# State space stage of a two-layer decoder: exponentials left in PSUM banks, matrix products on VectorE, terms on GpSimd

## The chip, the cores and the metric

The kernel runs on one core of one Trainium2 chip. The metric is the device time of one execution in microseconds. The kernel before was timed in three runs: 2670.41, 2675.45 and 2675.78 us, median 2675.45 us. The profile is of one more execution.

## What is computed

A decoder of two layers works on x, 16 batches of 256 tokens by 256 features in fp32, with a layer norm after every sublayer. The sublayers are: differential self attention, cross attention, a mixture of experts, a state space layer (Mamba-2 style), causal cross attention and a LoRA feed forward. The change touches the state space layer alone:

```python
zxbcdt = jnp.einsum('bld,ed->ble', x, in_proj_w)      # z 512, xBC 768, dt 8
xBC = silu(causal depthwise conv(xBC, 4 taps) + conv_b)
dt = softplus(dt + dt_bias);  A = -exp(A_log)          # 8 heads of 64, state of 128
...
def step(state, inp):
    x_t, B_t, C_t, dt_t = inp
    decay = jnp.exp(A[None, :] * dt_t)
    state = state * decay[:, :, None, None] + (x_t * dt_t[:, :, None])[..., None] * B_t[:, None, None, :]
    y_t = jnp.einsum('bhpn,bn->bhp', state, C_t)
...
y = (y + x_part * D) * silu(z)
y = y * rsqrt(mean(y * y) + EPS) * norm_w
x = layernorm(x + y @ out_proj_w.T)
```

## The kernel before

The recurrence is not stepped. With a = A dt, the output of a batch is y[t] = sum over s <= t of exp(a[s+1] + ... + a[t]) (B[s] . C[t]) dt[s] x[s]. For each batch and head the kernel makes the matrix of these factors and multiplies the scaled rows by it. The 256 tokens make two blocks of 128, so there are three blocks of matrix (first by first, first by second, second by second), and the eight heads are cut in two halves of four. That gives six units u = 0 to 5 a batch: block u // 2, half u % 2. Every unit is 128 x 512.

A unit goes through these steps. `high_terms` and `low_terms` multiply a triangle by a, split in an upper part `a_hi` and a rest `a_lo`, one tile of 128 x 1024 for each block of tokens (q = 0, 1); these are `rhs_hi` (VectorE) and `rhs_lo` (GpSimd). `exponents(n, u)` (TensorE) sums them by two matmuls into one of two banks, `e_ps[u % 2]`. `decays(n, u)` (ScalarE) takes the exponential from the bank and writes it to `mat[:, u]` in SBUF. `matrices(eng, n, u, ready)` multiplies `mat[:, u]` in place by `gm`, the masked products B . C, on VectorE for u = 0, 2, 4 and on GpSimd for u = 1, 3, 5. `mix(n, blk)` (TensorE) multiplies the scaled rows `xdt` by `mat`. A bank is free again once ScalarE has read it, and the same two banks also carry the transposed rows (`to_rows`) from which `scaled_rows` makes `xdt`.

Around it runs the rest of the layer. Inputs are projected for two batches at a time in eleven units (B, C, x0, x1, x2, dt, x3, z0 to z3) into two other banks, `in_ps`: six units in the even step, five in the odd. `project(n, i)` waits in `free_bank` until the unit two before it has been read out of its bank: for B, C and x units by the third tap of the convolution on VectorE (`taps`), which follows `first_tap` on ScalarE. `time_steps` and `exponent_terms` make dt and `a_hi`, `a_lo` for a pair of batches in the odd step; `copy_steps` (ScalarE) and `turn_steps` (TensorE) bring the dt unit to rows. Ahead of that, GpSimd gathers the expert rows of a batch by four indirect DMAs (`gather`), VectorE sums them and takes row moments (`sum_experts`), GpSimd makes the inverse root and `c_shift` (`scale_x`), ScalarE normalizes (`normalize_x`), and TensorE transposes the rows. Behind it, `output` multiplies by the output weights, `mean_squares`, `scale_rows`, `residual`, `row_moments`, `scale_y` and `normalize_y` finish a batch, and `skip_terms`, `gated`, `upper_y`, `square_y` and `split_y` lie between `mix` and the next step's `output`.

The order is written out by hand: each engine has a loop over the steps n = -7 to 16, with one order for even and one for odd n, and every engine runs its queue strictly in that order, with semaphores between the engines. A step handles batch n (`now`), finishes batch n - 1 (`late`) and prepares n + 1 (`soon`), while projections run for the pair that starts at n + 2, `normalize_x` for n + 4, `scale_x` for n + 5 and `gather` for n + 7. What can't be read from the diff is ScalarE's order in an even step, which doesn't change:

```python
first_tap(n, 0); decays(n, 0); first_tap(n, 1); normalize_x(n + 4)
decays(n, 1); decays(n, 2); tails(n); decays(n, 3)
first_tap(n, 2); decays(n, 4); first_tap(n, 3); decays(n, 5); first_tap(n, 4)
split_x(n + 4); upper_y(n); square_y(n); normalize_y(n - 1); copy_steps(n)
```

TensorE's order in an even step is `project(n, 0)`, `state_products`, `exponents` 0 and 1, `project(n, 1)`, `exponents` 2 and 3, `project(n, 2)`, `exponents` 4 and 5, `project(n, 3)`, `output(n - 1)`, `mix`, `project(n, 4)`, `transpose_x`, `to_rows(n + 1)`, `project(n, 5)`; the odd step has `turn_steps` ahead of its projections, and two of them between the exponents.

## Time and profile before

| What | us |
|---|---|
| median of three runs (2670.41 to 2675.78) | 2675.45 |
| the profiled execution | 2671.63 |
| its span, first to last instruction | 2669.9 |
| VectorE, GpSimd, ScalarE, TensorE busy in the span | 1950.1, 1619.4, 1423.5, 2341.5 |
| products with the mask, L2827, on VectorE (48 of them), median of one | 0.790 |
| the same on GpSimd (48), median of one | 1.312 |
| exponentials, L2670, ScalarE (96), median of one | 0.594 |
| first and last exponential of the stage start at | 1654.1, 2018.4 |

The mean granted clock of TensorE is 0.937 of full speed over the span. In the trace PE is TensorE, DVE is VectorE, ACT is ScalarE, POOL is GpSimd. Instructions overlap a little at their ends, so that from the start of one to the start of the next can be less than its duration. In a merged row, x2 says that two instructions in a row are counted, and the time is that of both. Idle time before a row stands in brackets, with what ended it.

### The profile page before, as it was taken

How to read it: one execution, taken by the hardware profiler on the slowest of the kernel's cores; microseconds unless marked ns; L12 is line 12 of the kernel's file. 1: busy time of each engine (PE TensorE's matmuls, PEld its weight loads, DVE VectorE, ACT ScalarE, POOL GpSimd, SP SyncE). 2: the span in 40 equal slices, each digit the busy share in tenths (PEclk: the TensorE clock that was granted, in tenths of full speed). 3: DMA queues.
4: the chain of work that ended last, by engine and by line, in shares of the span. 5: the costliest groups of instructions: out<-in, count | busy, mean ns of one | idle time of the engine just before them, and what ended most of it. 6: DMA issues, size and time to landing. Idle time of an engine off the chain costs nothing. (4 is left out here: it accounts for less than half of the span.)

```text
span 2669.9 us, 63255 instructions
## 1 busy us (share of the span) xinstructions
PE 2341.5 (88%) x23480; PEld 1968.6 (74%) x23480; DVE 1950.1 (73%) x3223; ACT 1423.5 (53%) x2223; POOL 1619.4 (61%) x1937
## 2 busy tenths in 40 slices
PE   5999999997799877998999965988995899987998
PEld 4677777775566656998999964777774666756998
DVE  2677777776589872646888857999984588875776
ACT  2566666664466652335666544655652466653333
POOL 3667666764467751275666656777764587863443
PEclk9899999999899987999999987998996799988999
DMA  8566666551889841146666652111002887841111
GB/s 205 131 159 159 160 145 158 153 120 43 245 216 229 219 111 36 52 138 204 224 228 226 230 175 64 41 48 32 21 13 85 213 225 208 224 105 41 53 54 52
DMA packets 227288, 363.44 MB, mean 136 GB/s; under 512 B 51968, under 2 KB 156416, under 8 KB 219520
## 3 DMA queue, kind: packets, MB, share of 16 engines
q1 hardware_dynamic: 207392, 281.32, 39.7%
q0 software_dynamic: 17376, 78.13, 8.6%
q8 instruction: 143, 2.34, 0.4%
q10 hardware_dynamic: 2304, 1.05, 0.2%
q14 instruction: 73, 0.60, 0.1%
HBM read 231.72 MB, written 133.69 MB: 137 GB/s over the span
## 5 line engine op out<-in xcount | busy, mean ns | idle before, releaser
L1369 ACT ACTIVATE self_probs<-self_score_ps 128x768 f32<-128x768 f32 x256 | 208.7, 815 | 183.9 <-PE self_score_ps L1271 182.0
L1585 POOL TENSOR_SCALAR_AFFINE_SELECT self_probs<-self_probs 128x512 f32<-128x512 f32 x256 | 169.5, 663 | 158.6 <-ACT self_probs L1369 158.6
L1506 DVE TENSOR_REDUCE self_neg_max<-self_max_ps 128x2 f32<-128x256 f32 x256 | 108.1, 422 | 165.1 <-PE self_max_ps L88 165.1
L647 ACT ACTIVATE cross_probs<-cross_score_ps 128x1024 f32<-128x1024 f32 x128 | 131.2, 1025 | 101.6 <-PE cross_score_ps L545 100.0
L745 DVE TENSOR_REDUCE cross_neg_max<-cross_max_ps 128x4 f32<-128x1024 f32 x128 | 154.9, 1212 | 39.1 <-PE cross_max_ps L524 39.0
L1507 DVE TENSOR_REDUCE self_neg_max<-self_max_ps 128x2 f32<-128x512 f32 x256 | 174.5, 682 | 0.0
L2297 POOL TENSOR_TENSOR moee_h_lo<-moee_h,moee_h_hi 128x512 fp32r<-128x512 f32 x78 | 112.5, 1442 | 92.3 <-ACT moee_h_hi L2034 91.6
L739 DVE TENSOR_REDUCE causal_block_max<-causal_max_ps 128x6 f32<-128x768 f32 x128 | 120.9, 946 | 56.4 <-PE causal_max_ps L88 55.9
L3592 POOL TENSOR_TENSOR ffn_g_lo<-ffn_g_full,ffn_g_hi 128x512 fp32r<-128x512 f32 x64 | 82.1, 1283 | 129.2 <-ACT ffn_g_hi L3478 116.9
L2034 ACT ACTIVATE moee_h_hi<-moee_h 128x512 fp32r<-128x512 f32 x110 | 69.6, 632 | 163.2 <-DVE moee_h L2200 163.2
L647 ACT ACTIVATE causal_probs<-causal_score_ps 128x768 f32<-128x768 f32 x128 | 103.6, 809 | 99.2 <-PE causal_score_ps L545 99.0
L79 PE MATMUL moee_g_ps<-moee_x_hi,moee_in_hi 128*128 128x256 f32 x440 | 131.3, 298 | 10.0 <-DVE moee_x_lo L2187 5.8
L1271 PE MATMUL self_score_ps<-self_q_stack,self_k_stack 49*128 49x128 f32 (+1 forms) x1024 | 129.0, 330 | 10.0 <-ACT self_probs L1369 6.4
L2200 DVE TENSOR_TENSOR moee_h<-moee_u_ps,moee_silu 128x512 f32<-128x512 f32 x110 | 75.5, 686 | 82.0 <-PE moee_u_ps L81 77.4
L2240 POOL DMA_INDIRECT x_tiles<-kept_x,moek_slot x64 | 65.8, 1029 | 107.1 <-issue 104.1
L79 PE MATMUL moee_y_ps<-moee_out_hi,moee_h_hi 128*128 128x256 f32 x440 | 125.4, 285 | 0.7 <-DVE moee_out_lo L2152 0.7
L81 PE MATMUL moee_g_ps<-moee_x_hi,moee_in_lo 128*128 128x256 f32 x440 | 125.7, 286 | 0.0
L79 PE MATMUL moee_u_ps<-moee_x_hi,moee_in_hi 128*128 128x256 f32 x440 | 125.7, 286 | 0.0
L80 PE MATMUL moee_g_ps<-moee_x_lo,moee_in_hi 128*128 128x256 f32 x440 | 125.7, 286 | 0.0
L80 PE MATMUL moee_u_ps<-moee_x_lo,moee_in_hi 128*128 128x256 f32 x440 | 125.1, 284 | 0.0
L81 PE MATMUL moee_u_ps<-moee_x_hi,moee_in_lo 128*128 128x256 f32 x440 | 125.1, 284 | 0.0
L81 PE MATMUL moee_y_ps<-moee_out_hi,moee_h_lo 128*128 128x256 f32 x440 | 124.9, 284 | 0.0
(507 smaller groups left out, 9479.9 us busy)
## 6 DMA issues: line engine op xcount, KB each, us to landing
self_q<-self_q_split SPq DMA_DIRECT2D x48, 512.0 KB, 3.5
self_q_raw<-self_q SPq DMA_DIRECT2D x32, 768.0 KB, 8.2
cross_stacks<-cross_qk SPq DMA_DIRECT2D x64, 384.0 KB, 6.4
causal_stacks<-causal_qk SPq DMA_DIRECT2D x64, 384.0 KB, 6.4
moe_y_tiles<-lasting_y_out SPq DMA_DIRECT2D x55, 256.0 KB, 2.5
mid<-lasting_y_out SPq DMA_DIRECT2D x48, 256.0 KB, 2.2
x_tiles<-zeros SPq DMA_DIRECT2D x16, 624.0 KB, 5.5
moee_xT<-x_tiles SPq DMA_DIRECT2D x39, 256.0 KB, 7.3
```

The lines of the kernel that those rows point to most:

```text
L79: pe.matmul(out, a[0], b[0], start=start, stop=False, **kw)
L80: pe.matmul(out, a[0], b[1], start=False, stop=False, **kw)
L81: return pe.matmul(out, a[1], b[0], start=False, stop=stop, **kw)
L647: nc.scalar.activation(probs[i // 2][:, a, :, lo:], score_ps[:, :, lo:], ACT.Exp, scale=HD ** -0.5).then_inc(prob_ready, 1)
L739: last = dve.tensor_reduce(block_max[:, :, col % 4, :], bank[:, :, 0:3 * P].rearrange("p a (j t) -> p a j t", t=P), AX.X, ALU.max, negate= ...
L745: last = dve.tensor_reduce(neg_max[p][:, tile, :, col % 4, :], bank[:].rearrange("p a (q k) -> p a q k", q=QT), AX.X, ALU.max, negate=True)
L1271: last = pe.matmul(score_ps[:, ab, j * S + k * P:(j + 1) * S], k_stack[p][rows, tile, k * P:(k + 1) * P], q_stack[rows, 4 * tile + c, k * P:],
L1369: nc.scalar.activation(probs[g % 4][:, a, :, P:], score_ps[:, :, P:], ACT.Exp, scale=HD ** -0.5).then_inc(prob_ready, 1)
L1506: dve.tensor_reduce(neg_max[:, tile, :, c, 0:1], bank[:, :, 0:P], AX.X, ALU.max, negate=True)
L1507: dve.tensor_reduce(neg_max[:, tile, :, c, 1:2], bank[:, :, S:2 * S], AX.X, ALU.max, negate=True).then_inc(max_kept, 1)
L1585: pool.affine_select(diagonal, diagonal, [[0, 2], [0, 2], [1, P]], ALU.is_ge, zero, base=0, channel_multiplier=-1).then_inc(prob_masked, 1)
L2297: pool.tensor_tensor(h_lo[p][f][:].rearrange("p j s -> p (j s)"), h[f][:], h_hi[p][f][:].bitcast(F32).rearrange("p j s -> p (j s)"), ALU.s ...
```

## The change

- `decays` writes the exponential back to its own bank instead of to `mat`, and no longer waits for `mix` of the batch before.
- `matrices` is VectorE's alone, for all six units. It reads the bank and `gm` and writes `mat[:, u]`; the first of a batch waits for `mix` of the batch before.
- The two counters `low_mat_ready` and `high_mat_ready` become one, `mat_ready`. TensorE's `exponents` (u >= 2) and `to_rows` now wait for it, that is for VectorE's reading of the bank, where they waited for ScalarE's.
- `high_terms` is taken from VectorE; GpSimd makes both rows of terms in `terms`, upper ahead of lower for each q, in the places of `low_terms`. GpSimd makes no product any more.
- VectorE's order changes: in an even step the products stand in pairs ahead of, between and behind the first two chunks of taps, and `sum_experts` moves from the head of the step behind `tail_rows`; in an odd step the products stand in pairs too.

```diff
@@ -2518,7 +2518,7 @@
                 if u >= 2:
-                    pe.wait_ge(decay_ready, 6 * n + u - 1)
+                    pe.wait_ge(mat_ready, 6 * n + u - 1)
                 else:
@@ -2530,7 +2530,7 @@
                     if b:
-                        pe.wait_ge(decay_ready, 6 * b - 1 + q)
+                        pe.wait_ge(mat_ready, 6 * b - 1 + q)
                     for f in range(FT):
@@ -2541,7 +2541,7 @@
                     pe.wait_ge(yd_ready, 2 * n - 1 + blk)
-                pe.wait_ge((low_mat_ready, high_mat_ready)[blk], 3 * n + 3)
+                pe.wait_ge(mat_ready, 6 * n + 5 + blk)
                 t = xdt[n % 2]
@@ -2665,10 +2665,7 @@
                 act.wait_ge(e_done, 6 * n + u + 1)
-                if u == 0 and n:
-                    act.wait_ge(ssm_done, 2 * n)
-                nc.scalar.activation(mat[:, u, :, :].rearrange("p h t -> p (h t)"), e_ps[u % 2][:],
-                                     ACT.Exp).then_inc(decay_ready, 1)
+                nc.scalar.activation(e_ps[u % 2][:], e_ps[u % 2][:], ACT.Exp).then_inc(decay_ready, 1)
 
@@ -2821,12 +2818,6 @@
 
-        def matrices(eng, n, u, ready):
-            eng.wait_ge(decay_ready, 6 * n + u + 1)
-            eng.wait_ge(gm_ready, n + 1)
-            eng.tensor_tensor(mat[:, u, :, :], mat[:, u, :, :],
-                              gm[:, u // 2, :].unsqueeze(1).broadcast_to([P, 4, P]), ALU.mult).then_inc(ready, 1)
-
         @block.vector
@@ -2923,19 +2914,10 @@
 
-            def high_terms(b):
-                if b:
-                    dve.wait_ge(e_done, 6 * b)
-                for q in range(QT):
-                    dve.tensor_tensor(rhs_hi[:, q, :, :], upto.unsqueeze(1).broadcast_to([P, NH, P]),
-                                      a_hi[:, b % 2 * QT + q, :].bitcast(F32).unsqueeze(2).broadcast_to([P, NH, P]),
-                                      ALU.mult).then_inc(rhi_ready, 1)
-
             def masked_products(n):
                 dve.wait_ge(g_done, n + 1)
                 if n:
-                    dve.wait_ge(low_mat_ready, 3 * n)
-                    dve.wait_ge(high_mat_ready, 3 * n)
+                    dve.wait_ge(mat_ready, 6 * n)
                 dve.tensor_tensor(gm[:], g_ps[:, 0:S + P].rearrange("p (b t) -> p b t", t=P), gmask,
@@ -2978,6 +2960,16 @@
                 moments(b, y_out[p], stats, mv[p], stat_ready, mean_ready)
+
+            def matrices(n, u):
+                dve.wait_ge(decay_ready, 6 * n + u + 1)
+                if u == 0:
+                    dve.wait_ge(gm_ready, n + 1)
+                    if n:
+                        dve.wait_ge(ssm_done, 2 * n)
+                dve.tensor_tensor(mat[:, u, :, :], e_ps[u % 2][:].rearrange("p (h t) -> p h t", t=P),
+                                  gm[:, u // 2, :].unsqueeze(1).broadcast_to([P, 4, P]),
+                                  ALU.mult).then_inc(mat_ready, 1)
 
@@ -3008,20 +3000,21 @@
                 if n % 2 == 0:
+                    if now:
+                        masked_products(n)
+                        matrices(n, 0)
+                        matrices(n, 1)
+                    taps(n, 0)
+                    if now:
+                        matrices(n, 2)
+                        matrices(n, 3)
+                    taps(n, 1)
+                    if now:
+                        matrices(n, 4)
+                        matrices(n, 5)
+                        tail_rows(n)
                     if real(n + 5) and n != -2:
                         sum_experts(n + 5)
-                    if now:
-                        masked_products(n)
-                    taps(n, 0)
-                    taps(n, 1)
-                    if now:
-                        matrices(dve, n, 0, low_mat_ready)
-                        matrices(dve, n, 2, low_mat_ready)
-                        tail_rows(n)
-                    if n >= 0 and soon:
-                        high_terms(n + 1)
-                    if now:
-                        matrices(dve, n, 4, low_mat_ready)
                     taps(n, 2)
@@ -3048,17 +3041,20 @@
                         masked_products(n)
+                        matrices(n, 0)
+                        matrices(n, 1)
                     if real(n + 5):
                         sum_experts(n + 5)
                     if now:
-                        matrices(dve, n, 0, low_mat_ready)
-                        matrices(dve, n, 2, low_mat_ready)
+                        matrices(n, 2)
+                        matrices(n, 3)
                         tail_rows(n)
                     taps(n, 0)
+                    if now:
+                        matrices(n, 4)
+                        matrices(n, 5)
                     if late:
                         mean_squares(n - 1)
-                    if now:
-                        matrices(dve, n, 4, low_mat_ready)
                     if late:
@@ -3073,7 +3069,6 @@
                         scaled_rows(n + 1)
-                        high_terms(n + 1)
 
@@ -3119,11 +3114,14 @@
 
-            def low_terms(b, q):
+            def terms(b, q):
                 if q == 0:
                     pool.wait_ge(alo_ready, b // 2 + 1)
                     if b:
                         pool.wait_ge(e_done, 6 * b)
+                pool.tensor_tensor(rhs_hi[:, q, :, :], upto.unsqueeze(1).broadcast_to([P, NH, P]),
+                                   a_hi[:, b % 2 * QT + q, :].bitcast(F32).unsqueeze(2).broadcast_to([P, NH, P]),
+                                   ALU.mult).then_inc(rhi_ready, 1)
                 pool.tensor_tensor(rhs_lo[:, q, :, :], upto.unsqueeze(1).broadcast_to([P, NH, P]),
@@ -3143,17 +3141,12 @@
                 now, late, soon = real(n), real(n - 1), real(n + 1)
-                if now:
-                    matrices(pool, n, 1, high_mat_ready)
-                    matrices(pool, n, 3, high_mat_ready)
                 if n % 2 == 0:
-                    if now:
-                        matrices(pool, n, 5, high_mat_ready)
                     if late:
                         scale_rows(n - 1)
                     if n >= 0 and soon:
-                        low_terms(n + 1, 0)
-                        low_terms(n + 1, 1)
+                        terms(n + 1, 0)
+                        terms(n + 1, 1)
                     if late:
@@ -3166,18 +3159,16 @@
                         scale_rows(n - 1)
-                    if now:
-                        matrices(pool, n, 5, high_mat_ready)
                     if n == -5:
                         scale_x(n + 5)
                     if n == -3:
                         scale_x(n + 5)
                     if soon:
-                        low_terms(n + 1, 0)
+                        terms(n + 1, 0)
                     if late:
                         scale_y(n - 1)
                     if soon:
-                        low_terms(n + 1, 1)
+                        terms(n + 1, 1)
                     if real(n + 7):
```

VectorE's queue, from the end of an odd step into an even one; `ssm_gm` is the masked product of `masked_products`, `ssm_bc` rows are `taps`, `ssm_mat` rows are `matrices`, `ssm_xdt_tail` is `tail_rows`. Before:

```order
L2859 BN_AGGR ssm_c_mv<-ssm_c_stats 128x2 x2
L2939 TENSOR_TENSOR ssm_gm<-ssm_g_ps,ssm_triang 128x384
L2893 SCALAR_TENSOR_TENSOR ssm_bc<-ssm_in_ps,ssm_cw,ssm_bc 128x2x255
L2893 SCALAR_TENSOR_TENSOR ssm_bc<-ssm_in_ps,ssm_cw,ssm_bc 128x2x254
L2893 SCALAR_TENSOR_TENSOR ssm_bc<-ssm_in_ps,ssm_cw,ssm_bc 128x2x253
L2893 SCALAR_TENSOR_TENSOR ssm_bc<-ssm_in_ps,ssm_cw,ssm_bc 128x2x255
L2893 SCALAR_TENSOR_TENSOR ssm_bc<-ssm_in_ps,ssm_cw,ssm_bc 128x2x254
L2893 SCALAR_TENSOR_TENSOR ssm_bc<-ssm_in_ps,ssm_cw,ssm_bc 128x2x253
L2827 TENSOR_TENSOR ssm_mat<-ssm_mat,ssm_gm 128x512 x2
L2947 TENSOR_TENSOR ssm_xdt_tail<-ssm_xdt,ssm_tail 128x512
L2930 TENSOR_TENSOR ssm_rhs_hi<-ssm_triang,ssm_a_hi 128x1024 x2
L2827 TENSOR_TENSOR ssm_mat<-ssm_mat,ssm_gm 128x512
```

With the change:

```order
L2937 TENSOR_TENSOR ssm_xdt<-ssm_e_ps,ssm_dt 128x512 x2
L2921 TENSOR_TENSOR ssm_gm<-ssm_g_ps,ssm_triang 128x384
L2970 TENSOR_TENSOR ssm_mat<-ssm_e_ps,ssm_gm 128x512 x2
L2884 SCALAR_TENSOR_TENSOR ssm_bc<-ssm_in_ps,ssm_cw,ssm_bc 128x2x255
L2884 SCALAR_TENSOR_TENSOR ssm_bc<-ssm_in_ps,ssm_cw,ssm_bc 128x2x254
L2884 SCALAR_TENSOR_TENSOR ssm_bc<-ssm_in_ps,ssm_cw,ssm_bc 128x2x253
L2970 TENSOR_TENSOR ssm_mat<-ssm_e_ps,ssm_gm 128x512 x2
L2884 SCALAR_TENSOR_TENSOR ssm_bc<-ssm_in_ps,ssm_cw,ssm_bc 128x2x255
L2884 SCALAR_TENSOR_TENSOR ssm_bc<-ssm_in_ps,ssm_cw,ssm_bc 128x2x254
L2884 SCALAR_TENSOR_TENSOR ssm_bc<-ssm_in_ps,ssm_cw,ssm_bc 128x2x253
L2970 TENSOR_TENSOR ssm_mat<-ssm_e_ps,ssm_gm 128x512 x2
L2929 TENSOR_TENSOR ssm_xdt_tail<-ssm_xdt,ssm_tail 128x512
```

The first two products now follow `ssm_gm` at once, and six tap instructions that stood ahead of every product stand behind them; `ssm_rhs_hi` is gone, and the sums of the experts, which ended at the first row of before, come after the last row.

GpSimd's queue in an odd step; `ssm_row_scale` is `scale_rows`, `ssm_var` to `ssm_shift` is `scale_y`, the DMAs are `gather`, `ssm_c_var` begins `scale_x`. Before:

```order
L3120 TENSOR_TENSOR ssm_row_scale<-ssm_ms,ssm_neg_half 128x2
L2827 TENSOR_TENSOR ssm_mat<-ssm_mat,ssm_gm 128x512
L3127 TENSOR_TENSOR ssm_rhs_lo<-ssm_triang,ssm_a_lo 128x1024
L3097 TENSOR_SCALAR ssm_var<-ssm_mv 128x2
L3098 TENSOR_SCALAR ssm_low<-ssm_mv 128x2
L3100 TENSOR_TENSOR ssm_rstd<-ssm_var,ssm_neg_half 128x2
L3102 TENSOR_TENSOR ssm_shift<-ssm_low,ssm_rstd 128x2
L3127 TENSOR_TENSOR ssm_rhs_lo<-ssm_triang,ssm_a_lo 128x1024
L3089 DMA ssm_y_routed<-moe_y_tiles,moek_slot 128x256 x4
L3097 TENSOR_SCALAR ssm_c_var<-ssm_c_mv 128x2
L3098 TENSOR_SCALAR ssm_c_low<-ssm_c_mv 128x2
```

With the change:

```order
L3115 TENSOR_TENSOR ssm_row_scale<-ssm_ms,ssm_neg_half 128x2
L3122 TENSOR_TENSOR ssm_rhs_hi<-ssm_triang,ssm_a_hi 128x1024
L3125 TENSOR_TENSOR ssm_rhs_lo<-ssm_triang,ssm_a_lo 128x1024
L3092 TENSOR_SCALAR ssm_var<-ssm_mv 128x2
L3093 TENSOR_SCALAR ssm_low<-ssm_mv 128x2
L3095 TENSOR_TENSOR ssm_rstd<-ssm_var,ssm_neg_half 128x2
L3097 TENSOR_TENSOR ssm_shift<-ssm_low,ssm_rstd 128x2
L3122 TENSOR_TENSOR ssm_rhs_hi<-ssm_triang,ssm_a_hi 128x1024
L3125 TENSOR_TENSOR ssm_rhs_lo<-ssm_triang,ssm_a_lo 128x1024
L3084 DMA ssm_y_routed<-moe_y_tiles,moek_slot 128x256 x4
L3092 TENSOR_SCALAR ssm_c_var<-ssm_c_mv 128x2
L3093 TENSOR_SCALAR ssm_c_low<-ssm_c_mv 128x2
```

A product has gone from behind `ssm_row_scale`, and each `ssm_rhs_lo` has an `ssm_rhs_hi` of the same size ahead of it, both pairs ahead of the gathers and of `scale_x`.

## Rows read from the trace of the kernel before

**Rows 1.** Windows view of one pair of batches: busy us of each engine, clock, DMA.
```profile
1752.00:1802.00 50.00, 43.79 (x306) 37.10 (x306) 47.99 (x88) 30.24 (x48) 38.42 (x40) 0.97 0.15 43
```

**Rows 2.** VectorE groups by shape, 1700 to 1990 us: busy, mean ns, idle before.
```profile
L2827 DVE TENSOR_TENSOR ssm_mat<-ssm_mat,ssm_gm 128x512 f32<-128x512 f32 x36 | 40.0, 1133 | 3.2 <-ACT ssm_mat L2670 2.9
L2930 DVE TENSOR_TENSOR ssm_rhs_hi<-ssm_triang,ssm_a_hi 128x1024 fp32r<-128x1024 f32 x22 | 30.3, 1417 | 1.8 <-PE ssm_e_ps L2527 1.8
```

**Rows 3.** GpSimd groups by shape, 1700 to 1990 us.
```profile
L2827 POOL TENSOR_TENSOR ssm_mat<-ssm_mat,ssm_gm 128x512 f32<-128x512 f32 x36 | 52.1, 1460 | 29.5 <-ACT ssm_mat L2670 28.5 <-DVE ssm_gm L2939 0.6
L3127 POOL TENSOR_TENSOR ssm_rhs_lo<-ssm_triang,ssm_a_lo 128x1024 fp32r<-128x1024 f32 x24 | 45.3, 1896 | 5.7 <-DVE ssm_a_lo L2924 5.7
```

**Rows 4.** Timeline of ScalarE, even step from 1752 us: start, us, instruction, wait.
```profile
1752.25 1.09 ACT L2731 ACTIVATE ssm_x<-ssm_x,ssm_c_shift,ssm_c_rstd 128x256 f32<-128x256 f32 x2 [1.73 <-POOL ssm_c_shift L3102]
...
1759.90 0.78 ACT L2689 ACTIVATE ssm_xs<-ssm_in_ps,ssm_cb,ssm_cw 128x512 f32<-128x512 f32 x1 [1.83 <-PE ssm_in_ps L81]
1760.58 0.59 ACT L2670 ACTIVATE ssm_mat<-ssm_e_ps 128x512 f32<-128x512 f32 x1
```

**Rows 5.** Timeline of GpSimd, odd step from 1788 us.
```profile
1788.46 1.90 POOL L3127 TENSOR_TENSOR ssm_rhs_lo<-ssm_triang,ssm_a_lo 128x1024 fp32r<-128x1024 f32 x1 [0.90 <-DVE ssm_a_lo L2924]
...
1792.66 1.90 POOL L3127 TENSOR_TENSOR ssm_rhs_lo<-ssm_triang,ssm_a_lo 128x1024 fp32r<-128x1024 f32 x1
1794.72 1.87 POOL L3089 DMA_INDIRECT ssm_y_routed<-moe_y_tiles,moek_slot  x1 [0.16 <-issue]
...
1802.04 0.18 POOL L3102 TENSOR_TENSOR ssm_c_shift<-ssm_c_low,ssm_c_rstd 128x2 f32<-128x2 f32 x1
```

**Rows 6.** Timeline of VectorE, from 1761 us.
```profile
1761.40 2.30 DVE L2893 SCALAR_TENSOR_TENSOR ssm_xs<-ssm_in_ps,ssm_cw,ssm_xs 128x510 f32<-128x510 f32 x3
...
1770.91 1.26 DVE L2955 TENSOR_TENSOR ssm_xdt<-ssm_e_ps,ssm_dt 128x512 f32<-128x512 f32 x2
1772.08 2.30 DVE L2893 SCALAR_TENSOR_TENSOR ssm_xs<-ssm_in_ps,ssm_cw,ssm_xs 128x510 f32<-128x510 f32 x3
...
1774.90 0.18 DVE L2905 TENSOR_TENSOR ssm_v<-ssm_in_ps,ssm_bias 128x32 f32<-128x32 f32 x1
...
1775.46 1.91 DVE L2867 SCALAR_TENSOR_TENSOR ssm_y_shared<-ssm_y_routed,moek_weight,ssm_y_shared 128x256 f32<-128x256 f32 x2
...
1780.45 0.68 DVE L2947 TENSOR_TENSOR ssm_xdt_tail<-ssm_xdt,ssm_tail 128x512 f32<-128x512 f32 x1
...
1783.35 2.37 DVE L2827 TENSOR_TENSOR ssm_mat<-ssm_mat,ssm_gm 128x512 f32<-128x512 f32 x1
1786.40 0.88 DVE L2971 SCALAR_TENSOR_TENSOR lasting_y_out<-ssm_xT_ps,ssm_row_scale,ssm_x 128x256 f32<-128x256 f32 x2 [0.68 <-issue]
...
1788.19 0.19 DVE L2924 TENSOR_TENSOR ssm_a_lo<-ssm_a,ssm_a_hi 128x32 fp32r<-128x32 f32 x1
...
1796.69 0.87 DVE L2867 SCALAR_TENSOR_TENSOR ssm_y_shared<-ssm_y_routed,moek_weight,ssm_y_shared 128x256 f32<-128x256 f32 x2
...
1799.47 0.52 DVE L2939 TENSOR_TENSOR ssm_gm<-ssm_g_ps,ssm_triang 128x384 f32<-128x384 f32 x1
```

**Rows 7.** Timeline of TensorE: exponents of even batches; output of an odd step.
```profile
1657.51 0.50 PE L2526 MATMUL ssm_e_ps<-ssm_rhs_hi,ssm_one_r 128*128 128x512 f32 x1 [1.86 <-ACT ssm_mat L2670]
...
1753.87 0.50 PE L2526 MATMUL ssm_e_ps<-ssm_rhs_hi,ssm_one_r 128*128 128x512 f32 x1 [3.72 <-ACT ssm_mat L2670]
...
1779.46 0.28 PE L79 MATMUL ssm_xT_ps<-ssm_wo_hi,ssm_y_hi 128*128 128x256 f32 x1
...
1783.95 0.28 PE L81 MATMUL ssm_xT_ps<-ssm_wo_hi,ssm_y_lo 128*128 128x256 f32 x1
...
1803.89 0.79 PE L2526 MATMUL ssm_e_ps<-ssm_rhs_hi,ssm_one_r 128*128 128x512 f32 x1 [3.72 <-ACT ssm_mat L2670]
...
1904.58 0.50 PE L2526 MATMUL ssm_e_ps<-ssm_rhs_hi,ssm_one_r 128*128 128x512 f32 x1 [1.87 <-ACT ssm_mat L2670]
...
1949.74 0.50 PE L2526 MATMUL ssm_e_ps<-ssm_rhs_hi,ssm_one_r 128*128 128x512 f32 x1 [0.90 <-ACT ssm_mat L2670]
```

2 lines of the change are left out of this document (1 added, 1 removed).

## Prediction

> **What bounds the stage now.** I read first the windows of one pair of batches (one even and one odd step): of 50.00 us VectorE is busy 47.99, TensorE 43.79, GpSimd 38.42, ScalarE 30.24 [rows 1]. VectorE is the fullest engine, so the next view is its groups by shape: 36 products with the mask at 1133 ns and 22 upper terms at 1417 ns on average [rows 2]. These means hide two prices. A product that meets GpSimd's own takes 2.37 us, where a free one takes about 0.7 [rows 6]. The reader sees an engine that is full and partly held up by GpSimd.
>
> The third view, the timelines, shows a second thing that an average can't: a ring through all engines that just fits into the 50 us. In an odd step VectorE ends `a_lo` at 1788.38 [rows 6]. GpSimd starts its lower terms behind it at 1788.46, does `scale_y`, the second lower terms at 1792.66, four gathers from 1794.72, `scale_x`, and ends `c_shift` at 1802.22 [rows 5]: 13.8 us. `normalize_x` of the next even step waits for that `c_shift` on ScalarE (1.73 us in the pair before, start at 1752.25) [rows 4]; behind it in ScalarE's queue stands the second exponential of that batch, and TensorE waited 3.72 us for it, to 1753.87, and again to 1803.89 [rows 7]. In between VectorE did other work, since its queue had ten independent things ahead of the first product; it lost nothing. I call the end of `c_shift` ahead of an even step T0 (1752.2, then 1802.2).
>
> **What the change does to busy time.** VectorE now does 12 products a pair instead of 6, each with one operand in a bank. The nearest row is `scaled_rows`, which multiplies a bank by a broadcast SBUF operand: two begin at 1770.91 and the next work at 1772.08, 0.59 us each [rows 6]. So 12 x 0.59 = 7.1 us. It drops 6 x 1.13 = 6.8 and 4 x 1.42 = 5.7 us [rows 2]. Net 5.4 us a pair less. GpSimd drops 6 products at 1.46 = 8.8 us and gains 4 upper terms, priced as its lower terms of the same shape, 1.90, so 7.6 us [rows 3]: about even. ScalarE's exponential keeps its 0.59 us [rows 4] in my sum. A write to a bank is not in this trace; I bound it by 0.4 and 0.8 us, and since only the second and sixth exponentials stand in the ring, that is +-0.4 us a pair. The Trainium skill ("ScalarE: Activation LUTs", the section on what each stage is for) says that ScalarE writes PSUM faster than SBUF and gives no figure; by it the sum would lie nearer the lower end, and no run shown here tests it.
>
> **What it does to the ring.** Three edits lengthen it.
> 1. GpSimd now makes upper and lower terms between `a_lo` and `c_shift`: 2 x 1.90 = 3.8 us more. Against that, the 1.87 us first gather [rows 5] lay beside VectorE's upper terms, and without them I take 1.0, and `scale_y` loses a stall of some 0.6 beside the gated product. 13.8 + 3.8 - 0.9 - 0.3 = 16.4 us.
> 2. VectorE's queue in an even step now has `matrices(n, 1)` ahead of all taps. It waits for the second exponential, so for `normalize_x`, so for T0. Nothing behind it can start: in-order. Hence all of VectorE's work up to `a_lo` follows T0 in series. `normalize_x` and the exponential take 1.7 us. Then, even step: five products 2.9, two chunks of taps 4.4, tail row 0.6, `sum_experts` 2.8 (1796.69 to 1799.47), and from the third taps to the end 13.5 less 0.4 of idle (1761.40 to 1774.90). Odd step: 0.6 to 1775.46, six products 3.5, `sum_experts` 2.8, tail row with taps 2.9 (1780.45 to 1783.35), residual to `a_lo` 2.0 (1786.40 to 1788.38) [rows 6]. Sum 1.7 + 23.8 + 11.8 = 37.3 us. With GpSimd's 16.4 the ring is 53.7 us if VectorE never waits otherwise, against 50.0.
> 3. It does wait. A bank is free only when VectorE has read it, and the products stand between the taps. Laid out from T0: second product done 2.4, first taps 4.6, two products 5.8, second taps 8.0, fifth product 8.6. TensorE may project `x1` only when the second taps have freed its bank, 8.0 to 9.4; `first_tap` 0.8 and the sixth exponential 0.6 [rows 4] end at 10.9, so VectorE stands 2.3 us before its sixth product. In the trace of before the same exponential already trails that `first_tap` (start 1760.58), but only GpSimd waited. GpSimd's four terms in a row (7.6 us) now lie beside `gated`, the tail row and `sum_experts`: I add 1.4 us for two meetings. The trace shows such meetings: two additions of `sum_experts` took 1.91 us at 1775.46 and 0.87 at 1796.69 [rows 6]. `scale_y` and `normalize_y` come behind these terms and ahead of `copy_steps`: 0.4 us at `time_steps`. In the odd step TensorE gets the banks of the last two exponent units only after `sum_experts`, starts `output` some 1.9 us later, and `output` lasts 4.8 us (1779.46 to 1784.23) [rows 7], so that `residual` waits another 1.3. Sum 5.4. Ring: 53.7 + 5.4 = 59 us.
>
> What hides the lost VectorE time otherwise: between `a_lo` and the next `matrices(n, 1)` VectorE has 6.6 us of work and then stands some 10 us for T0. Its 5.4 us saved go there, and give nothing back.
>
> **The sum.** From the second exponent matmul pair of batch 0 to that of batch 12 the trace has 1657.51 to 1949.74, 292.2 us [rows 7]. After: the first T0 comes 3.8 us of terms later, less the gather's 0.9, of which 1.7 us remain behind the wait that was there; the first ring has no older batch, 55.4; then three at 59, batches 2 to 8, 177.0; the ring from 8 to 10 has no gathers (-5.2) and is then held by the products themselves, 54.2; from 10 to 12 there is no `sum_experts` in the odd step and no `normalize_x` ahead, 51.8. Total 1.7 + 55.4 + 177.0 + 54.2 + 51.8 = 340.1, which is 47.9 us more. From batch 12 on neither taps of a new pair nor inputs remain, and I see gains and new waits of about 1 us that cancel: 0. Other stages are untouched. The profiled execution took 2671.63 us, 3.8 below the median of the three runs shown, so 2671.6 + 48 = **2720 us**. About 0.2% (5 us) is what a measurement of this kernel can tell from none.
>
> **Rivals.**
> *A cheaper ring, still slower.* If the waits of point 3 overlap, the ring is 53.7 us: three rings give 11, the first, fifth and sixth 0 to 2 each, the start 1.7, together 10 to 20 us: 2682 to 2692. For it: the layout above sums waits by hand, and one late engine often covers another. Against: the sixth product's wait has no cover.
> *VectorE's relief wins.* If T0 came before VectorE's queue reached the second product, the pair would shrink by up to 5.4 us, stopped by TensorE's 43.79 of 50 [rows 1], say 4.5 us over seven pairs: -31, 2640 us. It needs `a_lo` at most 33.6 us after T0 (50 less 16.4); before it was 36.2 (1752.2 to 1788.4), and VectorE's own work after T0 is 37.3. That is 3.7 us short of the turning point, so it needs GpSimd's upper terms at half my price. For it only: VectorE is 96% busy now and is what most waits lead to.
> *The shared port decides.* In this trace an instruction of VectorE with two SBUF operands waits for the end of GpSimd's (2.37 us, above). GpSimd's terms now fill 15.2 us a pair, so `gated`, two tail rows and four additions may each wait up to 1.9. At four full waits the ring is 59 + 6 = 65 us and the time 2672 + 72 = 2744. The Trainium skill ("SBUF — State Buffer", who interferes with whom) calls this an exclusive lock for the whole instruction, and says that a VectorE instruction with one SBUF input is exempt. The trace agrees on both: the free bank products of `scaled_rows` keep 1.26 us for two [rows 6].
>
> That the change isn't what it says can be left out: both listings show all twelve products on VectorE and all terms on GpSimd.
>
> **How the numbers follow.** Forecast (ring of 57 to 61 us, 2705 to 2730) 0.55; cheaper ring 0.18, of which 0.03 falls within 0.2%; port 0.12; relief 0.10; anything else near zero change 0.05. Slower 0.82, same 0.08, faster 0.10. The range 2683 to 2748 leaves out the relief and a little of either edge.
>
> **What would show it.** Right: the busy time of VectorE in the stage falls while its idle time before `ssm_mat<-ssm_e_ps` for ScalarE's exponential grows to several us, six times; `c_shift` to `c_shift` near 59 us over the middle pairs; TensorE idle before the exponents for VectorE's products; ScalarE's longest wait is `normalize_x` for `ssm_c_shift`; products near 0.68 us with hardly a spread. Wrong: pairs of 50 us or less, VectorE still over 90% busy, or products of over 0.8 us.

## The result, and the profile after

The changed kernel takes **2762.82 us** (median of 4 runs, 2755.97 to 2763.74) against 2674.36 us for the kernel before (the three runs above and a fourth): a ratio of 1.0329, 95% interval 1.0315 to 1.0344, so 88 us more. The forecast was 48 us more: it had the direction and the chain over `c_shift`, which I call the ring, but the result lies above its range. The profiled execution took 2763.59 us (span 2761.9), 92.0 more than that of before.

How long the **stage** takes is read from each trace in the same way: from the first statistics of an input batch (`ssm_c_mv`) to the first matmul of the next stage. Before it is 502.5 us, after 584.8: 82.3 more. Of the other 9.7 us, 7.8 lie ahead of the stage, in code that the change doesn't touch. The stage began anywhere between 1600.7 and 1610.1 us in the traces below, so I take those 7.8 for spread between executions. The stretches of the prediction, from the TensorE timeline of after (start and duration in us, engine, line, operation, count, idle before and its releaser), second exponent pair of batches 0, 2, 8, 10 and 12:

```profile
1666.65 0.53 PE L2526 MATMUL ssm_e_ps<-ssm_rhs_hi,ssm_one_r 128*128 128x512 f32 x1 [2.55 <-DVE ssm_mat L2970]
...
1727.50 0.79 PE L2526 MATMUL ssm_e_ps<-ssm_rhs_hi,ssm_one_r 128*128 128x512 f32 x1 [4.67 <-DVE ssm_mat L2970]
...
1912.30 0.79 PE L2526 MATMUL ssm_e_ps<-ssm_rhs_hi,ssm_one_r 128*128 128x512 f32 x1 [4.67 <-DVE ssm_mat L2970]
...
1970.58 0.65 PE L2526 MATMUL ssm_e_ps<-ssm_rhs_hi,ssm_one_r 128*128 128x512 f32 x1 [1.49 <-DVE ssm_mat L2970]
...
2026.15 0.51 PE L2526 MATMUL ssm_e_ps<-ssm_rhs_hi,ssm_one_r 128*128 128x512 f32 x1 [0.55 <-DVE ssm_mat L2970]
```

| stretch | before | forecast | after |
|---|---|---|---|
| start, inside the stage | 0 | +1.7 | +1.3 |
| batch 0 to 2 | 46.3 | 55.4 | 60.9 |
| 2 to 8, three rings | 151.6 (1703.82 to 1855.39) | 177.0 | 184.8 |
| 8 to 10 | 49.2 | 54.2 | 58.3 |
| 10 to 12 | 45.2 | 51.8 | 55.6 |
| 12 to the stage's end | 0 | +0 | +13.7 |

The windows view of one ring of after, from one `c_shift` to the next (columns as in [rows 1]):

```profile
1786.81:1848.41 61.60, 48.09 (x306) 37.80 (x306) 43.81 (x89) 30.51 (x48) 36.73 (x39) 0.89 0.12 35
```

VectorE's busy time fell from 47.99 [rows 1] to 43.81 us, the pair rose by 11.6. No engine is full: the pair is a chain. The waits of after from 1720 to 1840 (engine and line, what it waits for: total, times, longest) name its links:

```profile
POOL ssm_row_scale L3115 <- DVE ssm_ms L2944: 38.2, 4, 16.4
...
DVE ssm_mat L2970 <- ACT ssm_e_ps L2668: 20.5, 8, 4.8
...
PE ssm_e_ps L2526 <- DVE ssm_mat L2970: 13.5, 6, 4.7
...
ACT ssm_x L2728 <- POOL ssm_c_shift L3097: 6.1, 2, 3.0
...
PE ssm_xT_ps L2453 <- DVE lasting_y_out L2953: 4.6, 2, 2.3
DVE ssm_gm L2921 <- PE ssm_g_ps L2513: 4.6, 1, 4.6
```

ScalarE waits for `c_shift`, VectorE's product for ScalarE, TensorE's exponent for the product. This is the foreseen chain. The last two rows are not in my layout: in an even step TensorE's `transpose_x` stands 2.3 us for the `residual` of VectorE's queue, and VectorE 4.6 us for TensorE's `g_ps` ahead of the masked products. Step by step, first from the timelines of ScalarE and VectorE of after:

```profile
1786.84 1.09 ACT L2728 ACTIVATE ssm_x<-ssm_x,ssm_c_shift,ssm_c_rstd 128x256 f32<-128x256 f32 x2 [3.04 <-POOL ssm_c_shift L3097]
```
```profile
1788.45 0.69 DVE L2970 TENSOR_TENSOR ssm_mat<-ssm_e_ps,ssm_gm 128x512 f32<-128x512 f32 x1 [4.78 <-ACT ssm_e_ps L2668]
...
1799.13 0.69 DVE L2970 TENSOR_TENSOR ssm_mat<-ssm_e_ps,ssm_gm 128x512 f32<-128x512 f32 x1 [2.60 <-ACT ssm_e_ps L2668]
...
1810.07 2.82 DVE L2994 TENSOR_TENSOR ssm_yz<-ssm_yz,ssm_zs 128x1024 f32<-128x1024 f32 x1
...
1831.40 0.19 DVE L2915 TENSOR_TENSOR ssm_a_lo<-ssm_a,ssm_a_hi 128x32 fp32r<-128x32 f32 x1
...
1842.28 0.56 DVE L2921 TENSOR_TENSOR ssm_gm<-ssm_g_ps,ssm_triang 128x384 f32<-128x384 f32 x1 [4.57 <-PE ssm_g_ps L2513]
```

and GpSimd's leg, in the same view:

```profile
1831.69 1.89 POOL L3122 TENSOR_TENSOR ssm_rhs_hi<-ssm_triang,ssm_a_hi 128x1024 fp32r<-128x1024 f32 x1 [2.38 <-DVE ssm_a_lo L2915]
...
1841.84 1.08 POOL L3084 DMA_INDIRECT ssm_y_routed<-moe_y_tiles,moek_slot  x1 [0.16 <-issue]
...
1848.20 0.19 POOL L3097 TENSOR_TENSOR ssm_c_shift<-ssm_c_low,ssm_c_rstd 128x2 f32<-128x2 f32 x1
```

From T0 (1786.8) to the second product 1.6 us (forecast 1.7), to the sixth 12.3 (10.9), to the end of `a_lo` 44.8 (42.7), and GpSimd from there to `c_shift` 16.8 (16.4). The first gather costs 1.08 us, where I took 1.0.

### The profile page after: what moved, and what is told of

Read it like the earlier page. It is cut to its first block and busy times, and to the rows that moved or that the text cites. A ratio compares the mean times of both kernels' runs of the same rounds, so it can differ in the third digit from the quotient of the medians.

```text
span 2761.9 us, 63160 instructions
## 1 busy us (share of the span) xinstructions
PE 2372.3 (86%) x23480; PEld 1977.7 (72%) x23480; DVE 1920.2 (70%) x3239; ACT 1425.5 (52%) x2223; POOL 1606.5 (58%) x1921
## 5 line engine op out<-in xcount | busy, mean ns | idle before, releaser
L3583 POOL TENSOR_TENSOR ffn_g_lo<-ffn_g_full,ffn_g_hi 128x512 fp32r<-128x512 f32 x64 | 82.3, 1286 | 128.5 <-ACT ffn_g_hi L3469 116.1
L80 PE MATMUL moee_y_ps<-moee_out_lo,moee_h_hi 128*128 128x256 f32 x440 | 124.8, 284 | 0.0
```

The lines of the kernel that those rows point to most:

```text
L80: pe.matmul(out, a[0], b[1], start=False, stop=False, **kw)
```

## Experiments

Each kernel is the one named, with the shown edit alone. The table has what was measured. A pair is the mean of the three even steps from batch 4 to 10, from the masked products of one even step to those of the next. "Beside" is the kernel before in the same session. All but the last two kernels had one execution, so a total is known to some 8 us (the kernel before, 23 times in the last session, ran from 2661.34 to 2680.15), while the stage is steadier: one kernel profiled twice had 498.6 and 499.7. Its last part is the least steady: from the masked products of batch 14 to those of batch 15 the kernel before took 17.3 us and e7_before_norm_late, whose code is the same there, 20.4; e6_before_terms_pool and e14_terms_norm, also the same there, took 21.6 and 26.3. So a difference of under some 5 us between two stages says little.

| kernel | stage | pair | total | beside |
|---|---|---|---|---|
| before | 502.5 | 50.8 | 2671.63 | |
| after | 584.8 | 61.5 | 2763.59 | |
| e1_norm_late | 565.4 | 56.5 | 2745.17 | 2681.85 |
| e2_gather_late | 570.3 | 58.2 | 2743.31 | 2681.85 |
| e4_exp_to_sbuf | 581.6 | 62.7 | 2749.34 | 2681.85 |
| e5_taps_first | 582.0 | 59.8 | 2755.97 | 2681.85 |
| e8_sum_first | 571.8 | 59.2 | 2744.11 | 2673.78 |
| e9_sum_norm | 547.5 | 54.4 | 2725.56 | 2673.78 |
| e3_high_on_dve | 565.1 | 58.1 | 2736.07 | 2673.78 |
| e6_before_terms_pool | 527.0 | 55.4 | 2704.95 | 2673.78 |
| e12_and_steps | 568.3 | 58.8 | 2739.60 | 2674.24 |
| e14_terms_norm | 521.2 | 53.3 | 2698.15 | 2674.24 |
| e7_before_norm_late | 505.9 | 50.8 | 2676.86 | 2674.24 |
| e15_before_order | 529.3 | 54.3 | 2699.13 | 2674.24 |
| e16_sn_sbuf | 545.0 | 54.7 | 2716.71 | 2680.80 |
| e17_sn_high | 532.9 | 52.5 | 2703.85 | 2680.80 |
| e18_hybrid | 503.6 | 49.4 | 2673.63 | 2680.80 |
| e19_hybrid_norm | 498.6 | 48.3 | 2666.76 | 2680.80 |

**The ring over `c_shift`.** In the changed kernel, `normalize_x` of even steps late:

```diff
                     first_tap(n, 1)
-                    if real(n + 4):
-                        normalize_x(n + 4)
...
                         decays(n, 5)
+                    if real(n + 4):
+                        normalize_x(n + 4)
```

> The changed kernel with one move: in even steps ScalarE normalizes the rows of batch n + 4 behind the sixth exponential, not ahead of the second. The state space stage (first row moments to the first attention matmul behind it) took 502.5 us before and 584.8 us with the change. Theory A, the ring through c_shift: the second exponential no longer waits for T0, but it still stands behind the first tap of unit C, which ended 2.4 us ahead of T0. So the second product starts some 2.5 us after T0 less 5, that is 2.5 us earlier, in six steps, and TensorE's wait there falls from 4.7 to about 2.2 us: 15 to 20 us less, stage 565 to 570. Rival B, bank release and product order alone set the pair: no wait moves but TensorE's by under 1 us a pair, stage 578 or more. Rival C, the shared port: no change, 585.

19.4 us of stage less, as my theory said. But the pair stays at 56.5 us: with `c_shift` out of it there is a second ring, nearly as long. Its links are the two that I had not laid out (waits of e1 from 1720 to 1960):

```profile
DVE ssm_mat L2970 <- ACT ssm_e_ps L2668: 23.0, 16, 2.5
...
DVE ssm_gm L2921 <- PE ssm_g_ps L2513: 18.2, 4, 4.6
...
PE ssm_xT_ps L2453 <- DVE lasting_y_out L2953: 9.2, 4, 2.3
```

The same ring, shortened instead of cut: in odd steps GpSimd issues its gathers behind `scale_x`.

```diff
-                    if real(n + 7):
+                    if n < -1 and real(n + 7):
                         gather(n + 7)
                     if n >= -1 and real(n + 5):
                         scale_x(n + 5)
+                    if n >= -1 and real(n + 7):
+                        gather(n + 7)
```

> The changed kernel with one move: from step -1 on, GpSimd's four gathers of an odd step stand behind scale_x. c_shift comes 5.2 us earlier. Theory A: the same 2.5 us a pair as with the late normalization, since then the first tap of unit C bounds the second exponential, so stage 565 to 570, and both experiments agree within 3 us. If they agree, T0 is worth that much and no more of the 82 us. Rival B or C: 578 or more.

14.5 us less, 3.3 us a middle pair, though the four gathers took 5 us ahead of `scale_x`; 4.9 us of stage fewer than with `normalize_x` late, so the two don't agree as closely as A had it. Both say that the c_shift ring holds the changed kernel by no more than 3 to 5 us a pair.

**Banks.** Exponentials go to SBUF as before, ScalarE frees the bank, VectorE multiplies all six in place:

```diff
-                nc.scalar.activation(e_ps[u % 2][:], e_ps[u % 2][:], ACT.Exp)...
+                nc.scalar.activation(mat[:, u, :, :]..., e_ps[u % 2][:], ACT.Exp)...
-                    pe.wait_ge(mat_ready, 6 * n + u - 1)
+                    pe.wait_ge(decay_ready, 6 * n + u - 1)
-                dve.tensor_tensor(mat[:, u, :, :], e_ps[u % 2][:]...
+                dve.tensor_tensor(mat[:, u, :, :], mat[:, u, :, :],
```

> The changed kernel with its exponentials written to SBUF again: ScalarE frees the bank, VectorE makes all six products in place in SBUF, in the order of the change, terms on GpSimd. Theory B, that the bank held until VectorE reads it costs most: TensorE no longer waits for products (43 us of waits in the stage), stage 545 or less. Theory A: order and T0 stay, only 0.6 us at the fourth exponent unit and some 1.9 us at the fifth in odd steps are won, partly hidden, and products with two SBUF operands meet GpSimd's terms: stage 565 to 585, products 0.7 to 1.0 us on average.

3.2 us less, and the middle pairs no shorter: taken together, who holds the bank is not what the change costs. But the sum is made of two parts. From the masked products of batch 14 on this kernel is 8.9 us shorter than the changed one, and ahead of them 5.7 us longer, with products of two SBUF operands that take 832 ns on average for 683. VectorE's taps in even steps ahead of its second product:

```diff
                         matrices(n, 0)
-                        matrices(n, 1)
                     taps(n, 0)
-                    if now:
-                        matrices(n, 2)
-                        matrices(n, 3)
                     taps(n, 1)
                     if now:
+                        matrices(n, 1)
+                        matrices(n, 2)
+                        matrices(n, 3)
```

> The changed kernel with VectorE's even step reordered: first product, both chunks of taps, then products two to six, tail row. Theory A with its second part (what stands behind the second product is blocked until T0, and the sixth exponential waits for the second taps through TensorE's projection): the taps are done while VectorE waits for T0, the wait ahead of the sixth product goes, 3.5 to 5 us a pair over seven pairs, stage 550 to 562. Rival B (banks): TensorE's third exponent unit waits for nothing new, so the same. Rival C, the shared port and GpSimd's length: under 5 us, stage 580 or more.

A miss. I expected 3.5 to 5 us off each ring, and 2.8 us of stage came. From T0 (1780.3 in that trace) to the sixth product it is 10.9 us, 1.4 less than with the change. The taps do fill the wait for `c_shift`, but the fourth to sixth products then wait 6.6 us for their exponentials, where they waited 3.7: TensorE is busy without a gap there, at a mean granted clock of 0.57 from 1782.6 to 1789.6.

**The place of `sum_experts`.** The diff moves it, in even steps, from the head of VectorE's queue to behind `tail_rows`. Put back:

```diff
                 if n % 2 == 0:
+                    if real(n + 5) and n != -2:
+                        sum_experts(n + 5)
                     if now:
                         masked_products(n)
...
                         tail_rows(n)
-                    if real(n + 5) and n != -2:
-                        sum_experts(n + 5)
```

> The changed kernel with one block moved: in even steps VectorE adds the experts' tiles (2.8 us) at the head of its queue again, ahead of the masked products, where it now stands 4.6 us idle. Theory A (VectorE's queue is one serial chain that TensorE's exponents wait for, and that block now stands in it): 2.8 us less for each of seven pairs, the stage from 584.8 to about 565 us, the even pairs from 61.6 to 58.5-59. Theory B (the wait for GpSimd's c_shift ahead of the second product sets the pair, and what stands ahead of it or behind it is filled in elsewhere): within 5 us, stage 580-590, and VectorE only waits longer at the second product.

13.0 us less, between the two and nearer A. The block of 2.8 us stood in the chain, while VectorE idled 4.57 us ahead of the same step. With `normalize_x` late as well:

> The same block moved, and also ScalarE's normalize_x of even steps behind the sixth exponential (which by itself gave 19 us). Theory A (two rings: the one over c_shift, and VectorE's serial order with TensorE; both edits shorten different ones): both gains add up, stage about 545 us, pairs 53-54. Theory B (both edits free the same ring): no more than the larger one alone, stage 563-567.

547.5 us: the gains add up, there are two rings. VectorE's wait for `g_ps` is gone from the waits of this kernel. With both of these, the taps first, and ScalarE's `copy_steps` ahead of `normalize_y`:

> The changed kernel with four moves at once: the experts' additions at the head of even steps, normalize_x behind the sixth exponential, VectorE's first two taps ahead of the second product, and ScalarE's copy_steps ahead of normalize_y. Theory A (VectorE's queue, with 5 to 8 us of waits a pair left after the first two moves, is what the pair consists of): the moves take 2 of the 2.5 us before the sixth product and 0.6 before time_steps, pairs 51.5 to 53, stage 530 to 540 us. Theory F (what VectorE no longer waits, TensorE then waits): stage 545 us or more, as with the first two moves alone.

Theory A falls: 20.8 us more than without. The waits of e12 from 1720 to 1960:

```profile
DVE ssm_mat L2970 <- ACT ssm_e_ps L2668: 30.8, 17, 2.7
PE ssm_e_ps L2526 <- DVE ssm_mat L2970: 27.2, 14, 4.2
```

In the kernel without the two moves (e9) they are 20.0 and 5.5 us. I read it so: with two banks the exponents, exponentials and products of a step take turns, and once `c_shift` no longer holds the second product up, 4.4 us of taps ahead of it are a plain delay. The two moves were not tried one by one here.

**Both rows of terms on GpSimd.** From the changed kernel's side (upper terms back on VectorE, behind the additions in even steps and `scaled_rows` in odd ones):

```diff
-                pool.tensor_tensor(rhs_hi[:, q, :, :], ...
+                        high_terms(n + 1)
```

> The changed kernel with the upper terms back on VectorE (behind the experts' additions in even steps, behind scaled_rows in odd ones), GpSimd with the lower terms alone. Theory A: GpSimd's leg from a_lo to c_shift is shorter by 2.8 to 3.8 us, VectorE's chain longer by two terms of even steps (2.8 us), stage within 8 us of 584.8. Theory C (GpSimd's doubled terms hold VectorE up over the shared port and that is where the surplus of the pair comes from): the gated product falls from 2.8 to 1.3 us and the stage comes to 565 us or less.

and added alone to the kernel before (the same edit the other way):

> The kernel before with one part of the change: both rows of terms on GpSimd, the matrices and their order as before. Theory A (the order of VectorE's queue costs, the terms on GpSimd little): the middle pairs 50 to 52 us, total +5 to +12 us against the kernel before. Theory C (the terms on GpSimd are the costly part): pairs of 55 us or more, total +30 or more.

19.7 us back (565.1, where C allowed 565; the gated product down to 1220 ns), 24.5 added: theory C in both. This part is a quarter to 30% of the loss. Is it the later `c_shift`, or the lock? The second kernel with `normalize_x` late:

> The kernel before with both rows of terms on GpSimd (which alone cost 24.5 us of stage, pairs 54.8) and normalize_x of even steps behind the sixth exponential. Theory D (the terms cost only through the later c_shift, which normalize_x waits for and the second exponential stands behind): pairs back to 50 or below, total 2665 to 2685 us. Theory L (they cost through the lock: gated 1.80 for 1.22 us, additions 1.27 for 0.48): pairs 53 or more, total 2695 or more.

Only 5.8 of the 24.5 us go; theory L holds by both its numbers. VectorE's groups from 1720 to 1960 (busy us, mean ns of one, idle before), the kernel before first, then e14:

```profile
L3002 DVE TENSOR_TENSOR ssm_yz<-ssm_yz,ssm_zs 128x1024 f32<-128x1024 f32 x10 | 12.2, 1221 | 0.2
...
L2874 DVE SCALAR_TENSOR_TENSOR ssm_x<-ssm_y_routed,moek_weight,ssm_y_shared 128x256 f32<-128x256 f32 x16 | 7.0, 482 | 0.3
```
```profile
L2994 DVE TENSOR_TENSOR ssm_yz<-ssm_yz,ssm_zs 128x1024 f32<-128x1024 f32 x10 | 19.8, 1979 | 0.2
L2874 DVE SCALAR_TENSOR_TENSOR ssm_x<-ssm_y_routed,moek_weight,ssm_y_shared 128x256 f32<-128x256 f32 x16 | 19.7, 1270 | 0.3
```

The gated product rises from 1221 to 1979 ns, the addition from 482 to 1270. Over 10 and 16 of them that is 20 us in 240, about 4.5 us a pair. The pair rose by 2.5, though the upper terms left VectorE. I read the one as the cause of the other; no run takes the lock alone away. The same edit without the terms:

> The kernel before with normalize_x of even steps behind the sixth exponential. Theory A (VectorE, 96% busy, sets its pair; the wait for c_shift is covered): within 5 us of the kernel before. Rival (the c_shift ring already costs the kernel before something, since TensorE waits 3.7 us a pair there): 10 to 20 us faster.

505.9 us: in the kernel before the wait for `c_shift` is covered, as [rows 4, 7] were read.

**The order alone.** The kernel before, with who makes what untouched, and VectorE's even step in the changed order:

```diff
-                    if real(n + 5) and n != -2:
-                        sum_experts(n + 5)
                         masked_products(n)
+                        matrices(dve, n, 0, low_mat_ready)
                     taps(n, 0)
+                        matrices(dve, n, 2, low_mat_ready)
                     taps(n, 1)
-                        matrices(dve, n, 0, low_mat_ready)
-                        matrices(dve, n, 2, low_mat_ready)
+                        matrices(dve, n, 4, low_mat_ready)
                         tail_rows(n)
                         high_terms(n + 1)
-                        matrices(dve, n, 4, low_mat_ready)
+                        sum_experts(n + 5)
```

> The kernel before with only the order of VectorE's even steps changed to the changed kernel's: masked products first, each product behind its exponential and between the taps, the experts' additions behind tail_rows; who makes what is as before (GpSimd three products a step and the lower terms). Theory A (the order costs: VectorE then stands at its second product for the exponential behind c_shift, with nothing else in front): pairs of 55 us or more, total +30 or more. Rival (the order is harmless as long as products and exponentials stay split over engines and out of the banks; the cost is in the hand-over of banks): total +15 or less.

26.8 us of stage, 3.5 us a pair, total +24.9: the order alone costs, somewhat less than A had. Nearly all of it (25.5 us) lies ahead of batch 14. Waits from 1720 to 1960:

```profile
DVE ssm_mat L2827 <- ACT ssm_mat L2670: 18.6, 12, 2.4
...
PE ssm_e_ps L2526 <- ACT ssm_mat L2670: 13.9, 4, 4.0
PE ssm_xT_ps L2453 <- DVE lasting_y_out L2971: 11.4, 5, 2.3
```

VectorE's products now wait for ScalarE where they stood at most 0.2 us before, and TensorE's transposes wait for the `residual`, which they did not. The middle row is no growth: it was 14.0 us in the kernel before. So the waits that make up the rings are there without one bank product.

**What is left of the 82 us.** On top of additions first and `normalize_x` late, exponentials to SBUF once more:

> The changed kernel with the additions at the head of even steps and normalize_x late (stage 547.5 us), and now also the exponentials back in SBUF, so that ScalarE frees a bank and not VectorE's product. Theory H (with the two rings gone, the handing over of two banks through three engines is the chain that is left): stage 525 to 537. Theory L (VectorE is nearly full, and the lock with GpSimd weighs more than the wait for a bank): the products rise from 0.68 to 0.9-1.2 us, stage 547 or more.

545.0: neither number is reached, and again the sum hides two parts. From batch 14 on it is 10.4 us shorter than without the edit, ahead of that 7.8 us longer, with products of 804 ns. So the bank that VectorE holds does cost, at the end of the stage, and products in SBUF cost about as much before. And upper terms on VectorE:

> The same kernel (additions at the head, normalize_x late, 547.5 us), exponentials in the banks, and the upper terms back on VectorE. Theory L (GpSimd's doubled terms cost by the lock and by its longer leg, as they did in the kernel before, 24 us, and between the changed kernel and its variant, 20 us): stage 524 to 532. Rival (VectorE, 46.8 of 54.3 us busy, is full by then; 5.7 us of terms replace 5.4 us of locks): stage 543 or more.

532.9 us, just above theory L and far from its rival. What the terms cost, by the lock and by GpSimd's longer leg together, is real here too (14.6 us). So three edits bring the changed kernel from 584.8 to 532.9. Of the other 30 us, 22.5 lie ahead of the masked products of batch 14 and 7.9 behind them. The first part stays open: no run here isolates it. That kernel still has the products between the taps, which alone cost the kernel before 26.8 with the late additions, so I argue for that, without having shown it. The second part is about as long (6.1 to 8.1 us) in the four kernels below, which have of the change only bank products.

**The bank products without the rest.** The kernel before, in which only VectorE's three products of a step stay in the bank, the first ahead of the taps:

```diff
-                if u >= 2:
+                if u in (2, 4):
+                    pe.wait_ge(low_mat_ready, 3 * n + u // 2)
+                elif u >= 2:
                     pe.wait_ge(decay_ready, 6 * n + u - 1)
...
+                to = e_ps[0][:] if u % 2 == 0 else mat[:, u, :, :]...
+                nc.scalar.activation(to, e_ps[u % 2][:], ACT.Exp)...
```

> The kernel before with only VectorE's three products of a step made from the bank (exponentials 1, 3 and 5 of 1 to 6 stay in the bank, the others go to SBUF for GpSimd as before), and VectorE's first product ahead of its taps so that the bank is handed on. Theory A (the cheap part of the change is right: a product from the bank is 0.68 instead of 1.13 us, 2.7 us a pair off an engine that is 96% busy): pairs 47.5 to 49, total 2655 to 2668. Rival (the hand-over makes TensorE wait for VectorE's products, which stand in a full queue): 2675 or more.

> The same, with normalize_x of even steps behind the sixth exponential. Theory A (VectorE's own work sets the pair, the c_shift ring is covered): within 4 us of the one without. Rival (the bank products brought VectorE into the c_shift ring): 8 us or more faster than the one without.

The products fall from 1133 ns [rows 2] to 684 ns (VectorE's groups of e18 from 1720 to 1960):

```profile
L2834 DVE TENSOR_TENSOR ssm_mat<-ssm_e_ps,ssm_gm 128x512 f32<-128x512 f32 x30 | 20.5, 684 | 3.7 <-ACT ssm_e_ps L2675 2.6 <-issue 0.3
```

The pairs fall to 49.4 and, with `normalize_x` late, 48.3. The single totals were 7 and 14 us below the kernel before: the first 5.6 us above A's 2668, with pairs 0.4 us above A's 49, the second 6.9 us better than the first where A allowed 4. They were too good, as five rounds of the second kernel showed:

> The kernel of e19_hybrid_norm again, timed in five rounds against the kernel before. From its one look (2666.76 beside 2680.80, stage 498.6 against 502.5): ratio 0.994 to 0.999, that is 4 to 15 us faster.

2671.61 us (12 runs) against 2672.40 (23 runs): ratio as recorded 1.0005 (it isn't that of the two medians), interval 0.9992 to 1.0018. No difference, though the stage is again 2.8 us shorter (499.7); the expectation fails. The trace says where the gain went. From the masked products of batch 0 to those of batch 14 this kernel takes 331.2 us for 342.1, so 10.9 less, as the pairs promise. From there to the next stage it takes 117.9 for 109.8, 8.1 more. In batch 14, which has no taps and no additions beside it, TensorE stands 2.56 us for VectorE's product, where it stood 1.85 for ScalarE, and its granted clock is then 0.50 from 1987.7 to 1999.7. In the pairs TensorE now waits for VectorE about as much (15.7 us from 1720 to 1960) as it waited for ScalarE before (14.0):

```profile
PE ssm_e_ps L2528 <- DVE ssm_mat L2834: 15.7, 15, 1.4
PE ssm_in_ps L79 <- DVE ssm_bc L2900: 4.3, 5, 1.0
```

Then VectorE's second product between the first two taps, and `copy_steps` ahead of `normalize_y`:

> The same kernel, with VectorE's second product (unit 3 of even steps) between its first two taps, and ScalarE's copy_steps ahead of normalize_y. Theory A (TensorE's 14.4 us of waits for VectorE's products over five pairs are what is left): pairs from 48.3 to 47-47.5, 5 to 9 us faster than without the two moves. Rival (as with the taps moved in e12_and_steps, what one wait loses the next one takes): within 3 us of it, or slower.

2668.94 us (12 runs): ratio 0.9985, interval 0.9970 to 1.0000, stage 493.9. The first row above fell to 11.7 us, the pair only from 48.2 to 48.1, and the total is 2.7 us from the one without the two moves: the rival's case. This is the best version seen, and at most 0.3% better than the kernel before; I don't call it a win.

## Why the prediction was right or wrong

**What failed.** Two steps. The sum ended with "cancel: 0" from batch 12 on, and those batches took 13.7 us more, the largest single miss. And the ring over `c_shift` was taken for the only chain, though products, taps and `residual` make a second one, nearly as long. Below, term by term.

**The direction and the ring: right.** VectorE's busy time fell by 4.2 us a pair (forecast 5.4) and gave nothing back, since the pair is a chain through T0: `c_shift` to `c_shift` 61.6 us. The bounds on the new prices hold: the exponential into the bank takes 574 ns on average (first row, after), into SBUF 590 (before), from ScalarE's groups from 1650 to 2100:

```profile
L2668 ACT ACTIVATE ssm_e_ps<-ssm_e_ps 128x512 f32<-128x512 f32 x90 | 50.3, 574 | 28.0 <-PE ssm_e_ps L2527 27.3
```
```profile
L2670 ACT ACTIVATE ssm_mat<-ssm_e_ps 128x512 f32<-128x512 f32 x96 | 53.7, 590 | 12.7 <-PE ssm_e_ps L2527 11.8
```

So the rule of the Trainium skill ("ScalarE: Activation LUTs", the section on what each stage is for) has the sign right, and here it is worth 16 ns. The product from the bank was priced at 0.59 after `scaled_rows`; 0.68 is its length and about 0.6 its step. VectorE's groups of after, from 1720 to 1960:

```profile
L2970 DVE TENSOR_TENSOR ssm_mat<-ssm_e_ps,ssm_gm 128x512 f32<-128x512 f32 x48 | 31.5, 683 | 41.0 <-ACT ssm_e_ps L2668 40.6
L2994 DVE TENSOR_TENSOR ssm_yz<-ssm_yz,ssm_zs 128x1024 f32<-128x1024 f32 x8 | 18.5, 2308 | 0.1
```

**"It does wait" (point 3, 5.4 us a ring): too small.** 61.6 less the busy ring of 53.7 is 7.9. Where the layout fell short: the sixth product came at 12.3 and not 10.9 us, because TensorE, which has no gap from 1791.4 on until the projection ahead of it is done, ran at its lower clock there. The windows of after from the second exponent on:

```profile
1789.20:1796.20 7.00, 6.00 (x13) 4.29 (x14) 5.79 (x9) 1.94 (x3) 0.06 (x1) 0.50 0.00 0
```

The granted clock is 0.50, that is 1.2 GHz, behind an idle time of 4.68 us, and a matmul takes 0.63 us where it takes 0.40 at full clock. My layout had prices at full speed. The gated product met the terms and took 2.82 us for 1.22, and the odd one 1.79: 2.2 us more where I had set 1.4 for two meetings. With GpSimd's leg (0.4 over) and the sixth product (1.4 late) that is about the missing 2.5 us. GpSimd's timeline beside that product, which is VectorE's row at 1810.07 above:

```profile
1809.91 1.90 POOL L3122 TENSOR_TENSOR ssm_rhs_hi<-ssm_triang,ssm_a_hi 128x1024 fp32r<-128x1024 f32 x1
1811.77 2.88 POOL L3125 TENSOR_TENSOR ssm_rhs_lo<-ssm_triang,ssm_a_lo 128x1024 fp32r<-128x1024 f32 x1
```

VectorE's product ends 1.1 us after the upper term does, at 1812.89, and the lower term, which began in between, is 0.98 us longer than its free 1.90: each waited the other out. The rival of the shared port was underrated: not four full waits of up to 1.9 us a ring, but 1.6 and 0.6 us, and 20 to 24 us of stage together with the longer leg.

**The first ring (55.4, was 60.9).** I priced `sum_experts` there at 2.8 us. Behind the tail row it met the terms of the next batch: its first two additions took 4.15 us (they take 0.87 alone). VectorE has no gap from there to the next batch's masked products, so these 3.3 us are part of the 5.5.

```profile
1677.88 4.15 DVE L2858 SCALAR_TENSOR_TENSOR ssm_y_shared<-ssm_y_routed,moek_weight,ssm_y_shared 128x256 f32<-128x256 f32 x2
```

**The last stretches (54.2, 51.8, and "cancel: 0"): the largest miss,** 4.1 + 3.8 + 13.7 = 21.6 of the 34.4 us of stage that were missing. The first two belong to the second ring, which needs no `c_shift`: products between taps, taps ahead of `residual`, `residual` ahead of TensorE's transposes and exponents. e1 shows it at 56.5 us a pair; and from the masked products of batch 10 to those of batch 12, a pair that doesn't end in a wait for `c_shift`, the changed kernel takes 56.5 us and e1 57.1.

The 13.7 us are another thing. The prediction says that from batch 12 on no taps of a new pair remain. They do: the units of batches 14 and 15 are projected in steps 12 and 13, and batch 14 is the first without taps. Step 12 costs 5.4 us more than before (with its taps between the products), step 13 3.1 us less, and the step from batch 14 to 15, with no taps and no `c_shift`, 10.3 us more; the rest 2.3. (Counted so, from the masked products, it is 14.9 us, of which 1.1 lie ahead of the exponents of batch 12.) The masked products of batches 14 and 15, before and then after:

```profile
1994.96 0.54 DVE L2939 TENSOR_TENSOR ssm_gm<-ssm_g_ps,ssm_triang 128x384 f32<-128x384 f32 x1
2012.28 0.55 DVE L2939 TENSOR_TENSOR ssm_gm<-ssm_g_ps,ssm_triang 128x384 f32<-128x384 f32 x1
```
```profile
2072.50 0.56 DVE L2921 TENSOR_TENSOR ssm_gm<-ssm_g_ps,ssm_triang 128x384 f32<-128x384 f32 x1 [1.30 <-PE ssm_g_ps L2513]
2100.14 0.55 DVE L2921 TENSOR_TENSOR ssm_gm<-ssm_g_ps,ssm_triang 128x384 f32<-128x384 f32 x1
```

In between, the second exponent pair of batch 14, before and after, and the windows of TensorE's work behind it, two of after and one of before:

```profile
1995.91 0.47 PE L2526 MATMUL ssm_e_ps<-ssm_rhs_hi,ssm_one_r 128*128 128x512 f32 x1 [1.85 <-ACT ssm_mat L2670]
```
```profile
2078.20 0.77 PE L2526 MATMUL ssm_e_ps<-ssm_rhs_hi,ssm_one_r 128*128 128x512 f32 x1 [4.81 <-DVE ssm_mat L2970]
```
```profile
2078.00:2084.00 6.00, 5.25 (x15) 3.83 (x16) 3.21 (x6) 2.41 (x5) 0.00 (x0) 0.50 0.00 0
2084.00:2090.00 6.00, 6.00 (x29) 6.00 (x30) 0.97 (x3) 0.00 (x0) 1.09 (x2) 0.50 0.00 0
```
```profile
2002.00:2008.00 6.00, 6.00 (x75) 5.70 (x74) 3.56 (x8) 0.00 (x0) 3.81 (x3) 1.00 0.00 0
```

TensorE stands 4.81 us for the product where it stood 1.85, and then does `output` and the start of `mix` at half clock, with nothing left to cover it. The other kernels part the causes of that wait: 1.9 us with the order alone (e15, whose step takes 17.2 us), 2.6 with bank products alone (e18), 4.1 to 4.2 with both terms on GpSimd and products in SBUF (e4, e6, e14, e16), 4.8 with both. So the end of the stage pays for the terms and for the bank, not for the order. How much of the 10.3 us is the wait and how much the clock behind it stays open; e6 and e14 with the same wait differ by 4.7 us in this step.

**The rivals.** "Relief wins" needed `a_lo` within 33.6 us of T0; it came at 44.8. The cheaper ring asked that waits overlap, and they didn't. The range ended too low: its upper end was the port's case alone, though port and layout could both be short together.

**The lock.** The rule named ahead ("SBUF — State Buffer", who interferes with whom, in the Trainium skill) is borne out on both halves. The bank products take 683 ns on average, also the two from 1819.2 that lie beside GpSimd's `ssm_y_lo` (1.29 us for both); the gated product, with both operands in SBUF, takes 2308 for 1221 ns.

## What to carry to other kernels

Work that is moved to another engine is paid where it stands in that engine's queue, not by its busy time: look for what every engine behind the moved instruction waits for, and for a second ring of nearly the same length before the first is taken for the only one. Keep independent work (here the 2.8 us of additions) in front of the instruction that waits on another engine, where it fills a hole, and check by a trial of the order alone. Lay out the last rounds of a loop by themselves: what the middle covers stands bare there, and here it ate 8 of the 11 us that bank products had won. A stage that gets 3 us shorter in the trace isn't a faster kernel until a dozen runs say so.

## What was not expected of the hardware

The lock costs both sides, in turns: beside GpSimd's terms the gated product rose from 1221 to 2308 ns on average and two additions from 0.87 to 4.15 us, and GpSimd's lower terms, 1.90 us in a row of before, took 2.88 us behind such a product. One short instruction can so lose more than its own length, and the exchange of equal busy times between these engines wasn't an even trade here. TensorE's clock fell to 0.50 in an idle time of 4.7 us and stayed there for 7 us of work behind it, and for 12 us and more behind the 4.8 us of batch 14, so that a wait of TensorE is paid again in the matmuls behind it. The kernel before shows it too: behind the 3.72 us ahead of 1803.89 [rows 7] the granted clock is 0.50 until 1807, and that first matmul takes 0.79 us for 0.50. How long it lasts isn't set by the wait alone: with the same code and the same 4.2 us of wait in batch 14, the four windows of 4 us behind it have 0.63, 0.94, 1.00 and 1.00 in e6, and 0.50, 0.50, 0.50 and 0.87 in e14.
